# Row sums of transposed squares on VectorE, and ScalarE's x3 ahead of the root of the wide variance

## What is computed

```python
x1 = layernorm(x  + L0(x, adj))    # hypergraph conv, relu, wide layer norm over 512, hypergraph conv
x2 = layernorm(x1 + L1(x1, adj))   # mean aggregation, concatenation, linear, relu
x3 = layernorm(x2 + L2(x2, adj))   # three GCN layers, relu between them
x4 = layernorm(x3 + L3(x3, adj))   # aggregation, linear, relu, mask
```

```python
mu  = jnp.mean(r, axis=-1, keepdims=True)
var = jnp.var(r, axis=-1, keepdims=True)
h   = (r - mu) * rsqrt(var + 1e-5) * gamma + beta
```

## Time and profile before

| what | value |
|---|---|
| median of 3 runs | 1382.34 us (1382.14 to 1383.41) |
| the profiled execution, its own time | 1382.37 us |
| its span in the profile | 1380.6 us |
| mean granted TensorE clock | 0.999 of full speed |
| busy share PE, DVE, ACT, POOL | 99%, 85%, 81%, 75% |
| chain that ended last, by engine | PE 97%, ACT 1%, issue 1% |
| DMA | 54.45 MB, mean 39 GB/s |

### The profile page before, as it was taken

The page is one execution under the profiler, slowest core; times in us unless marked ns, Lnnn a source line. Parts: engine busy times, 40 slices in busy tenths (PEclk is TensorE's granted clock), DMA queues, the critical chain, the costliest instruction groups (busy, mean ns, idle before and its releaser), DMA issues.

```text
span 1380.6 us, 35393 instructions
## 1 busy us (share of the span) xinstructions
PE 1365.6 (99%) x10836; PEld 1324.6 (96%) x10836; DVE 1168.3 (85%) x4037; ACT 1115.1 (81%) x2584; POOL 1032.8 (75%) x1114
## 2 busy tenths in 40 slices
PE   8999999999999999999999999999999999999997
PEld 7999999999999999999999999999999999999996
DVE  8888888888888888888888888888888888888896
ACT  6777887888888878878878888888788788888776
POOL 5758778778788787787787787877877877878531
PEclk9999999999999999999999999999999999999999
DMA  4101211211211112111112111111121121121000
GB/s 144 36 20 24 47 44 29 47 43 29 44 35 40 44 28 47 44 28 47 43 29 47 36 35 44 28 47 44 29 47 44 29 47 43 28 45 34 2 24 32
DMA packets 45804, 54.45 MB, mean 39 GB/s; under 512 B 12208, under 2 KB 28080, under 8 KB 45616
## 3 DMA queue, kind: packets, MB, share of 16 engines
q1 hardware_dynamic: 45616, 52.19, 16.3%
HBM read 35.33 MB, written 16.83 MB: 38 GB/s over the span
## 4 chain that ended last, share of the span: by engine, by line
PE 97%; ACT 1%; issue 1%; DMA 0%; SPq 0%; DVE 0%; POOL 0%; ACTq 0%; DVEq 0%; POOLq 0%
PE psum L400 95%; PE psum L499 2%; DMA r_f<-w1T_in 0%; PE psum L443 0%; ACT x L1034 0%; SPq L305 0%; ACT tk L1203 0%; ACT h_hi L1015 0%; SPq L338 0%; ACT h_f L1039 0%; DVE n_st L1605 0%; DVE n_s L274 0%; DVE xbw_lo L1670 0%; SPq L342 0%; ACT w1T_hi L1015 0%
## 5 line engine op out<-in xcount | busy, mean ns | idle before, releaser
L1034 ACT ACTIVATE x<-n_s,n_shift,n_rstd 128x256 f32<-128x256 f32 x384 | 208.8, 593 | 4.7 <-DVE n_shift L1629 4.1
L222 POOL TENSOR_TENSOR h_lo<-h_f,h_hi 128x512 fp32r<-128x512 f32 x120 | 155.0, 1292 | 57.7 <-ACT h_hi L1015 56.8
L229 POOL TENSOR_TENSOR r_lo<-r_f,r_hi 128x512 fp32r<-128x512 f32 x123 | 157.3, 1293 | 43.5 <-ACT r_hi L1015 43.5
L2292 POOL TENSOR_TENSOR n_s<-tk,mask 128x512 f32<-128x512 f32 x60 | 62.4, 1041 | 156.2 <-DVE mask L1682 135.2
L1605 DVE BATCH_NORM_STATS2 n_st<-n_s 128x6 f32<-128x256 f32 x384 | 141.9, 412 | 2.2
L400 PE MATMUL psum<-v_hi,h_hi 128*128 128x256 f32 x512 | 137.8, 291 | 2.0 <-ACT h_hi L1015 2.0
L1039 ACT ACTIVATE h_f<-psum,columns 128x256 f32<-128x256 f32 x256 | 107.6, 472 | 35.1 <-PE psum L400 35.0
L400 PE MATMUL psum<-A_f,x 128*128 128x128 f32 x1024 | 135.3, 275 | 0.6 <-ACT x L1034 0.5
L400 PE MATMUL psum<-v_lo,h_hi 128*128 128x256 f32 x512 | 132.7, 281 | 0.0
L400 PE MATMUL psum<-gx_hi,w1T_hi 128*128 128x256 f32 x512 | 132.2, 281 | 0.0
L400 PE MATMUL psum<-gx_hi,w1T_lo 128*128 128x256 f32 x512 | 131.9, 280 | 0.0
(11 more groups left out here) (177 smaller groups left out, 5159.8 us busy)
## 6 DMA issues: line engine op xcount, KB each, us to landing
x_in<-x_in_dram SPq DMA_DIRECT2D x64, 256.0 KB, 2.8
out<-x SPq DMA_DIRECT2D x64, 256.0 KB, 2.0
at_in<-adjT SPq DMA_DIRECT2D x64, 128.0 KB, 2.3
dinv_b<-dinv_row SPq DMA_DIRECT2D x55, 128.0 KB, 4.1
dinv_row<-dinv SPq DMA_DIRECT2D x55, 1.0 KB, 3.1
x<-v_in SPq DMA_DIRECT2D x3, 256.0 KB, 5.8
n_s<-w2T_in SPq DMA_DIRECT2D x2, 256.0 KB, 3.0
r_f<-w1T_in SPq DMA_DIRECT2D x2, 256.0 KB, 5.1
```

What stands on the lines that cost most here:

```text
L222: return e.tensor_tensor(dst[1][:], src, f(dst[0][:]), ALU.subtract).then_inc(signal, 1)
L229: e.tensor_tensor(r_s[1][:, half], r_f[:, half], f(r_s[0][:, half]), ALU.subtract).then_inc(r_lo[h], 1)
L1034: last = act.activation(dst[:, g, :], nm.s[:, g, :], ACT.Identity, scale=nm.rstd[:, g:g + 1], bias=nm.shift[:, g:g + 1])
L2292: pool.tensor_tensor(n4.s[:], tk[:], bc(mask[:], [C, 2, D], 2), ALU.mult).then_inc(tk_masked, 1)
```

## The change

Three things, in the code of the diff:

1. **`squares(p)`** on TensorE, for pairs 0 to 60 (`p + 1 < LAST`, with `LAST = 62`): in place of the two fp32 matmuls, two transposes of `sq1` (128x128 each) against the identity, into columns 384 to 511 of the two banks of `P`. For pairs 61 to 63 nothing changes.
2. **`wide_var(p)`** on VectorE, for the same pairs: a new `add_columns(p)` first waits for the transposes and for `h_mean2`, sums the 128 columns of both graphs by one `tensor_reduce` in PSUM, and writes the two sums to where the matmuls put them. `wide_var` waits for it.
3. **`body(n)`** on ScalarE: `make_x3(n - 4)` stands ahead of `root_h(n - 1)` in place of behind it. `fill()` and `drain()` keep their order.

```diff
+        sq_added = sem("sq_added")
...
             def squares(p):
                 pe.wait_ge(sq_sum, upto(p))
+                if p + 1 < LAST:
+                    if p == 0:
+                        pe.wait_ge(eye_loaded, 16)
+                    for g in range(2):
+                        last = pe.transpose(psum[:, bank("P", p) + g, 3 * C:4 * C], sq1[:, g, :], ident[:])
+                    last.then_inc(pe_did["P"], 1)
+                    return
                 for g in range(2):
                     last = mm(psum[:, bank("P", p) + g, D + 2:D + 3], sq1[:, g, :], ones[:, 0:1], True, True)
                 last.then_inc(pe_did["P"], 1)
...
                 square_mean(n - 1)
                 round_GT(n)
+                make_x3(n - 4)
                 root_h(n - 1)
-                make_x3(n - 4)
                 round_p(n - 1)
...
+            def add_columns(p):
+                b = bank("P", p)
+                dve.wait_ge(pe_did["P"], upto(p))
+                dve.wait_ge(hm2, upto(p))
+                if begun(p - 1):
+                    dve.wait_ge(hv, upto(p - 1))
+                dve.tensor_reduce(psum[:, b:b + 2, D + 2], psum[:, b:b + 2, 3 * C:4 * C], AX_X, ALU.add).then_inc(sq_added, 1)
+
             def wide_var(p):
                 b = bank("P", p)
+                if p + 1 < LAST:
+                    add_columns(p)
+                    dve.wait_ge(sq_added, upto(p))
                 h_var = psum[:, b:b + 2, D + 4]
                 dve.wait_ge(hm2, upto(p))
```

## The result

The changed kernel takes 1396.57 us (median of 4 runs, 1395.35 to 1397.25) against 1382.34 us (4 runs). That is 14.2 us more; the ratio is 1.010, with a 95% interval of 1.0083 to 1.0118. The forecast was 1389.0 us, 6.7 more, with a range of 1379 to 1394: slower was right, the size was less than half of what was measured.

What follows compares the result with a forecast made beforehand. TensorE's queue set the 21.04 us period; after the change a 21.18 us loop through ScalarE, VectorE and GpSimd would. 55 x 0.14 = +7.7, room -0.4, fill -0.6: +6.7 on 1382.34, so 1389.0 us, range 1379 to 1394.

Steps and rivals of the forecast that it cites:

- one that never touches TensorE (through `GT`): Loop body: round_GT, x3, root_h, VectorE, r_hi, r_lo, GpSimd to GT, next round_GT; forecast 21.18 us a period.
- Two signs: ScalarE in the loop: round_GT would start within 0.05 us of the end of GT, with ScalarE idle before it.
- first step: the fill: Before the loop: six transposed pairs save 1.1 us at most; -0.6 us taken.
- Second: the period: In the loop: 21.18 us instead of 21.04, 0.14 more in each of 55 bodies, +7.7 us.
- the 0.4 of room: ScalarE, GT to round_GT: round_GT started 0.41 us after it could; the loop uses this up first, -0.4 us.
- The x1 loop: From squares over root_h and x1 to xT and the next squares: 21.00 us a period.
- the forecast case: The loop through GpSimd's GT sets the period: 1389.0 us, alone 1384 to 1394; chance 0.62.
- rival 1: The loop through x1 binds, not the one through GpSimd: 21.00 us a period, 1380.5 us; chance 0.20.
- the chance of "no change": Whole kernel: time between 1379.6 and 1385.1 us, within 0.2% of before; chance 0.24.
- Rival 2: TensorE's saving comes through whole: 61 x 0.18 to 0.22 us, so 1370 us; chance 0.12.
- Rival 3: VectorE: the new reduction is the bound; at 1.0 us it adds 0.15 to 0.2 a body, 1398 us; chance 0.04.
- rival 4: TensorE: the transposes do not overlap, two times 0.273 us; period 21.23, 1394 us; chance 0.02.

Runs made afterwards that it cites:

- the fill as before: The changed kernel, but pairs 0 to 5, in the fill, keep the matmuls and have no reduction: 1392.32 us.
- `low_A` late: The changed kernel with GpSimd's low_A(n - 1) moved behind the last step of body(n): 1393.02 us.
- four reorderings: The changed kernel with round_GT behind root_h, xb ahead of GT_lo, matmuls kept in pairs 0 to 5, wide_var ahead of n4's inversion and shift: 1378.42 us.

## Why the prediction was right or wrong

**Right.** What bounds: the move of x3 closes two loops, one that never touches TensorE (through `GT`) and one that returns to it through x1, and the period is the longer one. The links as forecast and as measured: `GT_hi` to `h_rstd` 1.53 and 1.53; to the root of n1 6.77 and 6.77; to `r_lo` 4.30 and 4.30; GpSimd 8.54 and 8.52, so the waits that were subtracted did go; the reduction 0.42 and 0.43, hidden behind x3 as said. "Right" was defined as periods of 21.1 to 21.25 and about 0.3 us of waiting before `H2` and `xT`; the usual period is 21.22, and about 0.4 us a body is waited. Two signs were off: `round_GT` starts 0.09 us behind `GT`, not within 0.05, and ScalarE is hardly idle before it, since the mean's square ends there.

**Wrong in size, first step: the fill.** "The six transposed pairs of the fill save 6 x 0.18 = 1.1 at most; the fill is less tightly packed, I take -0.6." It costs 3.4 us, an error of 4.0, more than half of the 7.6 us that were missing. This is the step that failed. The prediction priced the fill by TensorE's rows only, as if the cover of the loop (x3 ahead of `root_h`) were there too; but `fill()` keeps its old order, and x3 does not hide the reduction there. The trace shows TensorE waiting there 2.6 us in four waits, for p_f and for x among others, and three instructions of VectorE that are about 1 us longer, each behind one of GpSimd that started first. The run with the fill as before shows that the fill's six pairs are the cause: 3.4 us back at the first `squares`, and 4 to 5 us in the time. Which of their steps costs how much is open.

**Second: the period.** 21.18 was forecast, 21.24 is the mean of the 54. The hand-over from GpSimd to ScalarE takes 0.09 us, not 0.04 as taken from VectorE's, and irregular periods, more than 0.1 us above the usual one (3 of 54 before, 6 now), lift the mean over the usual 21.22. With 54 periods that is 3.2 us with the 0.4 of room that was subtracted.

**Third: behind the loop** the drain is 0.6 us longer, forecast at nothing. That is no finding: in the other runs, which do not change it, it takes from 113.7 to 115.6 us.

**The rivals.** The x1 loop was priced at 21.00; by the run with `low_A` late it is 21.12 to 21.15. So the forecast case and rival 1 were not 0.18 apart but 0.09, and the chance of "no change" rested on a sum too low by 0.06 at the mean's square and 0.07 between x1 and the next `squares`. Rival 2 (TensorE's saving whole) needed four reorderings to come half true. Rival 3 is excluded by the doubled reduction, and rival 4 by 0.14 us for two transposes: the 0.273 us of a record overlap. The Trainium skill's figure of about 275 ns (TensorE: Matmul & The Clock Gate, Part 4) agrees with the length of one record here and not with what a transpose takes from the queue; the trace decides.

## What to carry to other kernels

When a saving on the full engine comes with one more step on another, add up the loop that this step closes through all the other engines, from an instruction to itself one body later: here 21.21 us against TensorE's 20.82, and the busy shares (85%, 79%, 74%) show nothing of it. Then price the code outside the loop by its own order, since what hides a step in the body need not stand in the fill. And when two halves of a change cover for each other, time each alone: the moved x3 is worth about 11 us with the sums and costs 12 without. Last, a long wait need not be the one that sets the period: with `low_A` late TensorE still waited before `H2`, and the loop that held went through `xT`.

## What was not expected of the hardware

**Two-input instructions on VectorE and GpSimd wait for each other.** `wab_lo` took 0.68 us when it started first and 1.59 when GpSimd's `r_lo` was 0.24 us ahead of it; `v_lo` took 1.74 with `x2c` 0.09 us ahead. The Trainium skill, SBUF — State Buffer, in the section on its two separate sides, says that a VectorE instruction with two SBUF inputs and a GpSimd instruction that reads SBUF share a pair of ports under an exclusive lock, and that the later one is blocked for the whole of the earlier. The trace agrees in kind, for whichever of the two starts first. By that rule `wab_lo` would end at 25.64 + 1.29 + 0.68 = 27.61; it ended at 27.47. `v_lo` would end at 53.46 and ended at 53.33, and in the kernel before `r_lo`, the second there, would end at 26.04 + 1.29 = 27.33 and ended at 27.19. Each ends 0.13 to 0.14 us before the sum.

**Hand-overs differ by pair of engines.** In these rows VectorE to ScalarE took 0.04 us (n_mv to its root), GpSimd to ScalarE 0.09 (`GT` to `GT_hi`), and x1 to the first matmul of `xT`, behind a wait, 0.06 in about a third of the bodies of the changed kernel and 0.12 to 0.14 in most others. Where it is 0.06, `xT` holds TensorE about 0.06 longer, so from the end of x1 to the next `squares` it is 10.72 us in the median. In a loop that closes by a tenth of a microsecond each of them counts.

**Two transposes do not always hold TensorE equally long.** The two of `squares` hold it 0.14 us (920.36 to 920.50) in all 55 bodies, two of the fill 0.18 and four of `xT` 0.35. What makes the difference is not shown.
